# Three quads of tokens routed through the first layer's experts by index

## The reference

```
x = _layernorm(x + _L0_attn_ref(x, W_Q, W_K, W_V, W_O))
x = _layernorm(x + _L0_ffn_ref(x, gate_w, wg, wu, wd, sg, su, sd))
x = _layernorm(x + _L1_attn_ref(x, ...))      # a state-space block: in-projection, convolution, decays, out-projection
x = _layernorm(x + _L1_ffn_ref(x, ...))

def _L0_ffn_ref(...):                          # 32 experts of width 96, 6 for each token, shared width 192
    scores = jax.nn.sigmoid(x @ gate_w)
    topk_w, topk_i = jax.lax.top_k(scores, 6)
    topk_w = topk_w / (jnp.sum(topk_w, axis=-1, keepdims=True) + 1e-20)
    combine = jnp.sum(jax.nn.one_hot(topk_i, 32) * topk_w[..., None], axis=1)
    g = jnp.einsum('td,edf->tef', x, wg)
    u = jnp.einsum('td,edf->tef', x, wu)
    routed = jnp.einsum('tef,efd,te->td', jax.nn.silu(g) * u, wd, combine)
    return routed + jax.nn.silu(x @ sg) * (x @ su) @ sd
```

## Time and profile before

| what | value |
|---|---|
| time, median of three runs | 1666.55 us |
| the three runs | 1666.93, 1663.94, 1666.55 us |
| the profiled execution, first to last instruction | 1664.1 us |
| attention, to the first step's first matmul | 611.0 us |
| the 204 steps with all that lies in them | 1042.75 us |
| last norm and store | 10.4 us |
| PE / PEld / DVE / ACT / POOL busy | 97 / 84 / 68 / 46 / 38 % |

### The profile page before, as it was taken

The page is one execution under the profiler, slowest core; times in us unless marked ns, Lnnn a source line. Parts: engine busy times, 40 slices in busy tenths (PEclk is TensorE's granted clock), DMA queues, the critical chain, the costliest instruction groups (busy, mean ns, idle before and its releaser), DMA issues.

```text
span 1664.1 us, 29632 instructions
## 1 busy us (share of the span) xinstructions
PE 1607.4 (97%) x9944; PEld 1403.7 (84%) x9944; DVE 1131.1 (68%) x2877; ACT 764.6 (46%) x1889; POOL 628.7 (38%) x379
## 2 busy tenths in 40 slices
PE   7999999999999979999999999999999999999997
PEld 6988888898888868888888888888888888888886
...
GB/s 212 159 140 143 141 118 180 132 158 139 142 141 137 1 59 205 191 196 205 199 225 188 184 176 209 194 187 165 207 189 175 146 206 197 178 175 172 195 206 107
DMA packets 101241, 277.75 MB, mean 167 GB/s; under 512 B 13488, under 2 KB 17584, under 8 KB 100112
## 3 DMA queue, kind: packets, MB, share of 16 engines
...
...
## 4 chain that ended last, share of the span: by engine, by line
PE 60%; issue 14%; DVE 13%; POOL 6%; ACT 4%; DMA 1%; SPq 1%; POOLq 0%; DVEq 0%; ACTq 0%
PE psum L352 54%; POOL act_sb L578 4%; PE psum L1324 2%; DVE s_sb L1019 1%; PE psum L1335 1%; PE psum L1514 1%; POOL mix L600 1%; ACT p_sb L701 1%; PE psum L1314 1%; ACT kT_hi L660 1%; DVE s_sb L1017 1%; DVE kT_lo L913 1%; DVE pT_lo L1034 1%; DVE x L934 1%; DVE p_sb L1027 1%
## 5 line engine op out<-in xcount | busy, mean ns | idle before, releaser
L352 PE MATMUL psum<-xT_hi,gu_w 128*128 128x512 f32 x1616 | 550.3, 401 | 4.2 <-DVE act_sb L1082 4.0
L578 POOL TENSOR_TENSOR act_sb<-act_sb,comb 128x512 f32<-128x512 f32 x184 | 311.1, 1691 | 614.8 <-DVE act_sb L1082 614.6
L1082 DVE TENSOR_TENSOR act_sb<-psum,gated 128x512 f32<-128x512 f32 x204 | 140.7, 690 | 378.9 <-PE psum L352 372.6
L742 ACT ACTIVATE gated<-psum 128x512 f32<-128x512 f32 x204 | 122.2, 599 | 600.3 <-PE psum L352 597.8
L352 PEld LDWEIGHTS psum<-xT_hi,gu_w 128*128 128x128 f32 x1616 | 304.2, 188 | 78.0 <-DVE act_sb L1082 5.6
L352 PE MATMUL psum<-xT_lo,gu_w 128*128 128x512 f32 x808 | 319.6, 395 | 0.0
L352 PEld LDWEIGHTS psum<-d_w,act_hi 128*128 128x128 f32 x1632 | 221.5, 188 | 19.7 <-issue 2.1
L544 POOL TENSOR_TENSOR split_stage<-raw_stage,split_stage 128x768 fp32r<-128x768 f32 x56 | 103.1, 1840 | 354.2 <-ACT split_stage L650 354.2
L352 PE MATMUL psum<-d_w,act_hi 128*128 128x256 f32 x1632 | 227.7, 282 | 0.4 <-ACT act_hi L750 0.4
L352 PEld LDWEIGHTS psum<-xT_lo,gu_w 128*128 128x128 f32 x808 | 152.2, 188 | 28.8
L1088 DVE TENSOR_TENSOR act_lo<-act_sb,act_hi 128x512 fp32r<-128x512 f32 x204 | 148.8, 729 | 2.1 <-ACT act_hi L750 1.8
(11 more groups left out here) (203 smaller groups left out, 3473.6 us busy)
## 6 DMA issues: line engine op xcount, KB each, us to landing
gu_w<-w_split SPq DMA_DIRECT2D x204, 512.0 KB, 3.6
d_w<-w_split SPq DMA_DIRECT2D x204, 256.0 KB, 3.8
...
comb<-l_comb_dram SPq DMA_DIRECT2D x128, 64.0 KB, 3.1
```

What stands on the lines that cost most here:

```text
L352: last = nc.tensor.matmul(out_ap, w, m, start=start and n == 0, stop=stop and n == len(pairs) - 1, **kw)
L578: pool.tensor_tensor(act_sb[:, s % 2, :], act_sb[:, s % 2, :], comb[:, comb_block(s) % 2, :], ALU.mult).then_inc(comb_done, 1)
L742: act.activation(gated[to, s % 2, :], psum[0:to.stop - to.start, G_BANK, :], ACT.Silu).then_inc(gated_ready, 1)
L1082: dve.tensor_tensor(act_sb[r, s % 2, :], psum[r, G_BANK if packed(s) else U_BANK, :], gated[r, s % 2, :], ALU.mult).then_inc(t_ready, 1)
```

## The change

Quad 0 goes through the first layer as before. Quads 1 to 3 keep only their two shared tiles there, so the dense steps fall from 204 to 132. Their routed part is done by index. After the norm, the choice of experts gives each of the 1536 x 6 pairs of token and expert a row in a DRAM table `xs` (a region of 1536 rows for each of 32 experts, zeroed beforehand by 42 DMAs of 1.25 MB during the attention). POOL scatters x to these rows by 72 indirect DMAs of 128 rows, two (a *unit*) a tick, each unit only once the unit before has landed. Then 103 *blocks* of 128 rows run: SP reads the block's first row from a table, loads its expert's weights (`weights_load`, 320 KB, ring of 6) and its rows (`rows_load`, 128 KB, ring of 4); PE transposes the rows, multiplies in full float32 with the expert's gate and up weights and then the down weights; results go to DRAM `os` (`block_store`, 256 KB for two blocks). In the second layer's first steps POOL gathers the six result rows of each token (72 indirect DMAs) and DVE adds them to x with their weights: two units, four DMAs, a step for quads 1 and 2 over 12 steps from tick K0, and for quad 3 over 6 steps from K0+30; a gather waits for the buffer of four units before, not for the landing of the last one.

The loops now run over *ticks*: 32 dense ones (steps 0 to 29), 8 pauses without a step, 103 with a block each (from B0 = 40), then 104 dense ones (from K0 = 143). The state-space slots stand in `MARKS`: pair 0 has slots 0 to 8 in ticks 33 to 40 and slots 9 to 51 over 91 ticks of the blocks; pairs 1, 2 and 3 have slots 0 to 43 in 15, 19 and 19 ticks of the second layer and slots 44 to 51 in two more, so two to four slots a tick.

```diff
+def tiles_of(f, q):
+    return f["lead"] if f is L0 and q else f["tiles"]
+
+
+STEP_LIST = [(f, q, j) for f in LAYERS for q in range(QUADS) for j in range(tiles_of(f, q))]
...
-    n = QUADS * L0["tiles"]
-    if s < n:
-        return L0, s // L0["tiles"], s % L0["tiles"]
-    return L1, (s - n) // L1["tiles"], (s - n) % L1["tiles"]
...
+ROUTED_QUADS = range(1, QUADS)
...
+BLOCKS = (REGION * TOP + SLOT * (BLOCK - 1)) // BLOCK
...
+XB_RING, BW_RING, OUT_RING = 4, 6, 4
...
+BREAK = first_step(L0, QUADS - 1)
+PAUSES = 8
...
+TICKS = dense_ticks(0, BREAK) + [Tick(None, None, None, None)] * PAUSES + [Tick(None, None, None, n) for n in range(BLOCKS)] \
+    + dense_ticks(BREAK, STEPS)
+B0 = BREAK + LAG + PAUSES
+K0 = B0 + BLOCKS
...
+CHOICE = {1: 0, 2: 3, 3: 6}
+COUNTED = CHOICE[3] + 4
+WEIGHED = {1: 14, 2: 17, 3: 20}
...
+SCATTERED = 4
+UNITS_IN = 4
+GATHERED = [K0 + u // 2 for u in range(24)] + [K0 + 30 + u // 2 for u in range(12)]
+COMBINED = 2
...
+NORM = -6
+MARKS = (((NORM, 28), (0, 33), (4, 37), (8, 39), (9, B0 + 1), (52, B0 + 92)),
+         ((NORM, K0 + 9), (0, K0 + 12), (44, K0 + 27), (52, K0 + 29)),
+         ((NORM, K0 + 30), (0, K0 + 33), (44, K0 + 52), (52, K0 + 54)),
+         ((NORM, K0 + 55), (0, K0 + 58), (44, K0 + 77), (52, K0 + 79)))
+SLOTS_AT = {}
+for _p in range(PAIRS):
+    for (_v, _n), (_w, _m) in zip(MARKS[_p], MARKS[_p][1:]):
+        for _s in range(_v, _w):
+            SLOTS_AT.setdefault(_n + (_s - _v) * (_m - _n) // (_w - _v), []).append((_p, _s))
...
+            def zero(n):
...
+                sp.dma_start(dst.rearrange("p (a w) -> p a w", w=BANK), zeros[:].to_broadcast([P, ZERO_ROWS // P * D // BANK, BANK])) \
+                    .then_inc(xs_zeroed, 16)
...
+                    if k < ZEROED:
+                        zero(ZEROED * g + k)
...
+            def weights_load(n):
+                row = first_row_of(n)
+                if n == 0:
+                    sp.wait_ge(down_done, BREAK)
+                wait(sp, b_down_done, n - BW_RING + 1)
+                sp.dma_start(block_w(n), l0_w[bass.ds(region_of(row), 1)].rearrange("a p w -> p (a w)")).then_inc(w_loaded[n % BW_RING], 16)
+
+            def rows_load(n):
+                row = first_row_of(n)
+                if n == 0:
+                    for q in ROUTED_QUADS:
+                        sp.wait_ge(scattered[q], 16 * QUAD * TOP)
+                wait(sp, xb_turned, n - XB_RING + 1)
+                sp.dma_start(xb[:, n % XB_RING, :], xs[bass.ds(row, BLOCK)]).then_inc(tokens_loaded[n % XB_RING], 16)
+
+            def block_store(n):
+                i, pair = n % 2, n // 2
+                if i == 0 and n < BLOCKS - 1:
+                    return
+                a = n - i
+                sp.wait_ge(b_copied, n + 1)
+                sp.dma_start(os[a * BLOCK:(n + 1) * BLOCK].rearrange("(i p) d -> p i d", p=P),
+                             b_out[:, 2 * (pair % 2):2 * (pair % 2) + i + 1, :]).then_inc(b_stored[pair % 2], 16)
+
+            sp.wait_ge(xs_zeroed, 16 * ZEROED * (GROUPS - 1))
             gu_load(0)
...
+            def scatter(u):
+
+                q, v = ROUTED_QUADS[u // PAIRS_OF], u % PAIRS_OF
+                if u == 0:
+                    pool.wait_ge(xs_zeroed, 16 * ZEROED * (GROUPS - 1))
+                else:
+                    pool.wait_ge(scattered[ROUTED_QUADS[(u - 1) // PAIRS_OF]], 32 * ((u - 1) % PAIRS_OF + 1))
+                if v == 0:
+                    pool.wait_ge(placed, ROUTED_QUADS.index(q) + 1)
+                tile, ks = unit_rows(u)
+                for k in ks:
+                    pool.indirect_dma_start(xs, bass.IndirectOffsetOnAxis(ap=row_of[:, tile, k:k + 1], axis=0), x[:, FIRST_TILE + tile, :], None) \
+                        .then_inc(scattered[q], 16)
+
+            def gather(u):
+                if u == 0:
+                    blocks_stored(pool)
+                    pool.wait_ge(weighed, len(ROUTED_QUADS))
+                wait(pool, combined, u - UNITS_IN + 1)
+                tile, ks = unit_rows(u)
+                for j, k in enumerate(ks):
+                    pool.indirect_dma_start(og[:, u % UNITS_IN, j, :], None, os, bass.IndirectOffsetOnAxis(ap=back_of[:, tile, k:k + 1], axis=0)) \
+                        .then_inc(og_loaded[u % UNITS_IN], 16)
+
...
+            def block_turned(n):
+
+                act.wait_ge(xb_turned, n + 1)
+                if n >= 2:
+                    act.wait_ge(gu_ready, n - 1)
+                act.activation(xbT[:, n % 2].rearrange("p c t -> p (c t)"), psum[:, TURN_BANK, 0:DC * BLOCK], ACT.Copy).then_inc(xbT_ready, 1)
+
+            def block_gate(n):
+                h = slice(0, WIDTH)
+                act.wait_ge(gu_ready, n + 1)
+                wait(act, bt_ready, n - 1)
+                act.activation(b_gated[h, n % 2, :], psum[h, gu_bank(n), 0:P], ACT.Silu).then_inc(b_gated_ready, 1)
+
+            def block_copy(n):
+                act.wait_ge(b_down_done, n + 1)
+                pair, i = n // 2, n % 2
+                if i == 0:
+                    wait(act, b_stored[pair % 2], 16 * (pair // 2))
+                act.activation(b_out[:, 2 * (pair % 2) + i, :], psum[:, DOWN_BANK, 0:D], ACT.Copy).then_inc(b_copied, 1)
+
...
+            def combine_rows(u):
+
+                tile, ks = unit_rows(u)
+                to = x[:, FIRST_TILE + tile, :]
+                dve.wait_ge(og_loaded[u % UNITS_IN], 32 * (u // UNITS_IN + 1))
+                for j, k in enumerate(ks):
+                    ins = dve.scalar_tensor_tensor(to, og[:, u % UNITS_IN, j, :], mix_of[:, tile, k:k + 1], to, ALU.mult, ALU.add)
+                    if j == 0:
+                        chained(ins)
+                ins.then_inc(combined, 1)
+                dve.wait_ge(combined, u + 1)
+
+            def block_act(n):
+                h = slice(0, WIDTH)
+                dve.wait_ge(b_gated_ready, n + 1)
+                wait(dve, b_down_done, n - 1)
+                dve.tensor_tensor(b_act[h, n % 2, :], psum[h, gu_bank(n), P:2 * P], b_gated[h, n % 2, :], ALU.mult).then_inc(bt_ready, 1)
+
...
+            def block_turn(n):
+                pe.wait_ge(tokens_loaded[n % XB_RING], 16 * (n // XB_RING) + 32)
+                wait(pe, xbT_ready, n)
+                for c in range(DC):
+                    last = pe.transpose(psum[:, TURN_BANK, c * BLOCK:(c + 1) * BLOCK], xb[:, n % XB_RING, c * P:(c + 1) * P], ident[:])
+                last.then_inc(xb_turned, 1)
+
+            def block_gate_up(n):
+                pe.wait_ge(xbT_ready, n + 1)
+                pe.wait_ge(w_loaded[n % BW_RING], w_landed(n % BW_RING, n, BREAK))
+                wait(pe, bt_ready, n - 1)
+                w, h = block_w(n), slice(0, WIDTH)
+                for i in range(2):
+                    last = chain(psum[h, gu_bank(n), i * P:(i + 1) * P],
+                                 [(w[:, c * UP + i * WIDTH:c * UP + (i + 1) * WIDTH], xbT[:, n % 2, c, :]) for c in range(DC)])
+                last.then_inc(gu_ready, 1)
+
+            def block_down(n):
+                h = slice(0, WIDTH)
+                pe.wait_ge(bt_ready, n + 1)
+                wait(pe, b_copied, n)
+                pe.matmul(psum[:, DOWN_BANK, 0:D], b_act[h, n % 2, :], block_w(n)[h, DC * UP:DC * UP + D], start=True, stop=True).then_inc(b_down_done, 1)
+
...
+                if t.block is not None:
+                    n = t.block
+                    if n + 2 < BLOCKS:
+                        block_turn(n + 2)
+                    if n + 1 < BLOCKS:
+                        block_gate_up(n + 1)
+                    block_down(n)
+                if t.gate == BREAK:
+                    pe.wait_ge(xbT_ready, BLOCKS)
...
```

More of the change, by code:

```diff
@@ L55 @@
 ROW = 3 * P
+TOP_BYTES = 32512
 IN_JOBS = 10
@@ new lines, with region_of, dense_ticks @@
+assert XB_RING == PAIRS
+assert REGION == 3 * 512 and all(v * 171 >> 9 == v // 3 for v in range((LAST_ROW >> 9) + 1))
+def region_of(row):
+    return ((row >> 9) * 171) >> 9
+Tick = namedtuple("Tick", "gate high down block")
+BREAK = first_step(L0, QUADS - 1)
+PAUSES = 8
+def dense_ticks(a, b):
+    at = lambda s: s if a <= s < b else None
+    return [Tick(at(s), at(s - 1), at(s - LAG), None) for s in range(a, b + LAG)]
+TICKS = dense_ticks(0, BREAK) + [Tick(None, None, None, None)] * PAUSES + [Tick(None, None, None, n) for n in range(BLOCKS)] \
+    + dense_ticks(BREAK, STEPS)
@@ L488, in store, with first_row_of @@
                 sp.dma_start(out.rearrange("(i p) d -> p i d", p=P)[:, QUAD * q:QUAD * (q + 1), :], x[:, QUAD * q:QUAD * (q + 1), :]).then_inc(stored, 16)
+            rows_of = {}
+            def first_row_of(n):
+                key = n // 8
+                if key not in rows_of:
+                    if n == 0:
+                        sp.wait_ge(rows_known, 1)
+                    while len(rows_of) > 1:
+                        del rows_of[next(iter(rows_of))]
+                    _, rows_of[key] = nc.values_load_multi_w_load_instructions(
```

(19 more changed lines are left out.)

609 lines of the change are left out of this document (447 added, 162 removed).

## The result

The changed kernel takes 1823.61 us (median of four runs, 1820.29 to 1832.2), the kernel before 1665.24 us beside it: the ratio is 1.0955, with an interval of 1.0925 to 1.0985. I had forecast 1640.

The account below looks back on a forecast made before the run. Dense steps at PE's pace, 4.20 us each with little idle, were taken as the bound. 1013 us to the blocks' end + 565 + 7 + 42, then 10.4 and 2.4, gave 1640 us, 27 faster; range 1578 to 1715.

Parts of the forecast that it names:

- The removed steps: First layer's dense steps: 72 routed steps go, each worth its whole 4.20 us of PE time, 302 us in all.
- Attention +5: Last attention group: norms of quads 1 and 2 move in and cost 5 us, between 0 and 13; first step at 616.
- Ticks 0 to 25, 125 us: Quad 0's first-layer ticks: 108 us of steps plus three expert choices and DVE chores; tick 26 starts at 741.
- Indirect DMAs of 0.8 us and units of 3.5: POOL's scatters: 0.8 us an issue, 3.5 us a unit with one landing; 15 units stand behind quad 0's last combine.
- Rival 2: Scatters and gathers: an indirect DMA costs POOL 1.5 us, units 4.6, so 1690 us in total; chance 0.10.
- Blocks 210 us, near both floors: The 103 blocks: 210 us, between 202 and 345, near the floors of PE (202 us) and DMA engines (187 us).
- Rival 3: Blocks bound by DMA latency or bandwidth: 300 us of blocks, 1730 us in total; chance 0.08.
- Gathers 7 us: Second layer's gather ticks: four issues at 0.8 and a combine make 4.9 us against 4.20, 7 us in all.
- Density 42 us, between 0 and 99: Second layer's packed state-space slots: heads lose 11, 7 and 7 us, expert choice 5.5 three times; 99 if every loop closes.
- Rival 1: Second layer's packed slots: POOL and the other engines wait for each other, 99 us instead of 42, 1697 in total; chance 0.22.
- The wrong sign: Failure test for the whole forecast: if blocks take over 250 us, or density over 70, the change is slower, not faster.

## Why the prediction was wrong, point by point

- **The removed steps** (4.20 us each, no more bound than that): right. The last 19 steps, with nothing beside them, stand 4.2 us apart.
- **Attention +5**: 7.9, inside its bounds.
- **Ticks 0 to 25, 125 us**: 138. I had queued the landing wait behind the scatters only. It stands ahead of the next combine, and without it these ticks are 15 us shorter.
- **Indirect DMAs of 0.8 us and units of 3.5**: 1.0 and 3.95. With 15 units that is 7 us; the rest of the 17 is two units that landed late (2 and 3 us) and a first unit that started 7.6 us after tick 26 and not 2.6. Rival 2, with 1.5 us, was too high; by its own mark, waits for landing over 70 us, it does not hold (63.9).
- **Blocks 210 us, near both floors**: 219 to PE's last matmul of a block, the rest to K0 is the reload. Their DMA share was 0.91, as foreseen, at 288 GB/s, and the half weights show that the bytes cost 10 us. Rival 3, with 300 us, falls.
- **Gathers 7 us**: 29 in the total, 35 in the second layer. Four issues of 1.0 with 0.3 us between are 5.1 us of POOL a tick, with a combine 6.7 against 4.2. The term was also added up wrong: 0.7 us in seven and six ticks make 9, and the gathers stand in 18 ticks, not 13.
- **Density 42 us, between 0 and 99**: this is the step that failed. 752.2 less the 565 of work is 187 us; 29 to 35 go with the gathers, some 155 remain. Of my 42, the choice of experts was right (16.5; PE waited 18.3 us for it). The heads were not: I had given PE 4.8 to 5.6 us and POOL 6.2 to 6.4 for a head and taken the difference, a balance of loads that came to 25 us. PE waited 60.1 us for `mix_lo`. For with 2.3 to 2.9 slots a tick, some ticks contain a head's `mixes`, `mix_low` and products together, and then PE waits for the sum of them and not for the difference; with the heads' slots spread, those waits fell to 19.7 us. I also looked at only two kinds of chain, heads and choice. The norms (36 us of waits) and the convolutions (9) were in no term, nor was the clock. Rival 1 named the right mechanism, "the packed slots close the loop", but the same two omissions are in its price of 99. Its mark came true, if barely: over the whole run PE waits 60.1 + 20.7 us for `mix_lo` and `comb_tok`, just over 80.
- **The wrong sign** was called at "density over 70", which is what happened. My chances gave rival 1 0.22 because POOL was busy 38% before. A low busy share says nothing of a chain in which each engine waits for the last.
- **What stays open**: how these 155 us divide. Measured one at a time in the second layer, the heads' width on POOL gives 31, the spread head loop 23, the clock 13, and these overlap; the changes to spacing, order and norms together took 67 us off it. What remains there was not taken apart; neither was POOL's time beside DVE's scans, 2.7 us of the 8.2 us chain in tick K0+67. A version that routes two quads, with pair 1 in dense steps, was not built.
